# Attention's second product with stationary values and moving probabilities in a decoder layer on one Trainium2 core

## What is computed

```python
x = x + self_attention(layernorm(x))              # causal, 16 heads of 8 channels
x = x + cross_attention_mlp(layernorm(x), ctx)    # attention over 64 rows of ctx, then 128 -> 256 -> 128, relu
x = x + rotary_attention_moe(layernorm(x))        # rmsnorm, causal attention, then 2 of 8 experts
```

```python
attn = softmax(S, axis=-1)        # over the keys
out = attn @ V                    # [queries, 8], 16 heads side by side give 128 channels
```

## Time and profile before

| | us |
|---|---|
| median of 3 runs (lowest to highest) | 653.37 (652.38 to 659.31) |
| the profiled execution, its own time | 655.04 |
| its span in the profile | 653.1 |
| PE busy (PEld busy) | 584.1 (457.8) |
| DVE busy | 470.1 |
| ACT busy | 380.2 |
| POOL busy | 262.0 |

### The profile page before, as it was taken

How to read it: one execution, slowest core, us unless ns; L and a number is a source line. 1 busy time by engine, 2 the same in 40 slices (tenths; PEclk the granted TensorE clock), 3 DMA queues, 4 the chain that set the end, 5 groups by cost and what they waited for, 6 DMA issues and landing times.

```text
span 653.1 us, 29845 instructions
## 1 busy us (share of the span) xinstructions
PE 584.1 (89%) x12373; PEld 457.8 (70%) x12373; DVE 470.1 (72%) x1134; ACT 380.2 (58%) x759; POOL 262.0 (40%) x370
## 2 busy tenths in 40 slices
PE   3789999989999998799998989997689998999990
PEld 1556667667676676576766657665589998999990
DVE  4648788787879779779897989989746673333562
ACT  3445566655656756466756565554457666676750
POOL 6100101010122124246446375655417877754451
PEclk9789899999999999799999999998889999999995
DMA  5231413120100100001011001010122222432445
GB/s 129 74 93 58 128 32 105 27 89 11 39 12 18 32 21 31 23 15 44 24 39 36 27 23 33 32 40 14 45 71 72 63 82 71 111 100 64 137 146 173
DMA packets 45267, 38.98 MB, mean 60 GB/s; under 512 B 11552, under 2 KB 37728, under 8 KB 45136
## 3 DMA queue, kind: packets, MB, share of 16 engines
q1 hardware_dynamic: 36736, 24.22, 13.1%
q0 software_dynamic: 4320, 8.92, 4.1%
q10 hardware_dynamic: 4080, 3.93, 2.0%
HBM read 18.75 MB, written 12.01 MB: 47 GB/s over the span
## 4 chain that ended last, share of the span: by engine, by line
PE 52%; DVE 21%; issue 10%; POOL 10%; DMA 4%; ACT 2%; SPq 1%; POOLq 0%; ACTq 0%; DVEq 0%
PE ps_s L820 9%; PE ring L1193 8%; PE ring L1155 7%; DVE rmax L1379 6%; PE ps_s L1181 6%; DVE shifted L1383 5%; PE ring L1209 5%; PE ring L828 4%; POOL moved_dram L1583 3%; PE ring L1054 3%; PE ps_s L1168 2%; PE ring L1063 2%; PE ring L1135 2%; POOL y_dram L784 2%; DVE stats L1403 2%
## 5 line engine op out<-in xcount | busy, mean ns | idle before, releaser
L1240 ACT ACTIVATE probsT<-ring 128x512 f32<-128x512 f32 x192 | 104.7, 594 | 137.7 <-PE ring L1193 137.4
L1379 DVE TENSOR_REDUCE rmax<-ps_s 128x16 f32<-128x1024 f32 x96 | 117.2, 1221 | 25.4 <-PE ps_s L1181 24.7
L1383 DVE TENSOR_TENSOR shifted<-ps_s,rmax 128x1024 f32<-128x1024 f32 x96 | 117.6, 1225 | 9.8
L1193 PEld LDWEIGHTS ring<-const,shifted 128*128 128x128 f32 x768 | 85.2, 144 | 43.7 <-issue 41.8
L1193 PE MATMUL ring<-const,shifted 128*128 128x128 f32 x768 | 109.1, 286 | 5.3 <-DVE room L1469 3.2
L912 DVE TENSOR_TENSOR room<-room,ps_s 128x384 f32<-128x384 f32 x71 | 39.3, 554 | 78.9 <-PE ring L828 57.1
L784 POOL DMA_INDIRECT y_dram<-room x71 | 70.2, 989 | 61.4 <-DVE room L917 48.6
L1209 PEld LDWEIGHTS ring<-vbd,probsT 128*32 128x32 f32 x6144 | 63.9, 111 | 43.9 <-issue 28.9
L820 PE MATMUL ps_s<-room 128*128 128x128 f32 x648 | 83.0, 279 | 1.1 <-issue 0.8
L1209 PE MATMUL ring<-vbd,probsT 128*32 128x18 f32 x6144 | 73.1, 187 | 8.6 <-issue 5.8
L820 PEld LDWEIGHTS ps_s<-room 128*128 128x128 f32 x648 | 78.3, 195 | 1.7 <-issue 1.7
(11 more groups left out here) (187 smaller groups left out, 925.1 us busy)
## 6 DMA issues: line engine op xcount, KB each, us to landing
room<-kS SPq DMA_DIRECT2D x96, 64.0 KB
room<-moved_dram SPq DMA_DIRECT2D x71, 65.0 KB, 1.9
room<-y_dram ACTq DMA_DIRECT2D x10, 256.0 KB, 3.2
room<-in_x SPq DMA_DIRECT2D x8, 256.0 KB, 4.6
cin<-in_ctx SPq DMA_DIRECT2D x8, 192.0 KB, 3.4
w_exp<-in_L_ffn_wg SPq DMA_DIRECT2D x8, 192.0 KB, 2.8
w_exp<-in_L_ffn_wu SPq DMA_DIRECT2D x8, 192.0 KB, 3.2
w_exp<-in_L_ffn_wd SPq DMA_DIRECT2D x8, 192.0 KB, 3.4
```

Of the source, the lines that this page charges most:

```text
L1193: last = nc.tensor.transpose(ring[u.bank][:, k * P:(k + 1) * P], flat[:, c:c + P], ident)
L1240: nc.scalar.activation(probsT[p % 2][:, 4 * g:4 * g + 4, :], ring[u.bank][:].rearrange("p (k c) -> p k c", c=P), ACT.Exp, scale=SCALE)\
L1379: V.reduce_max(rmax[p % 2][:].rearrange("p (g k) -> p g k", g=GROUPS), ps_s, AX.X).then_inc(rmax_ready, 1)
L1383: V.tensor_tensor(shifted[p % 2][:].rearrange("p (g k) s -> p g k s", g=GROUPS), ps_s, rmax[p % 2][:].rearrange("p (g k) -> p g k", g=GROU ...
```

## The change

`probsT` becomes the moving operand and `vbd` the stationary one, so that the result comes out with channels on partitions. The 128 channels are four quarters of 32, each written by its own column tile of PE; a quarter holds four heads, two head pairs ("sides"). `vbd` has for each sequence and quarter a period of 48 columns: 16 of one side's values, 16 zeros, 16 of the other side's. A window of 32 columns from the start or from the middle holds one side's values and zeros for the other, and the two sides accumulate. The sums no longer come from a column of ones in the values but from a second set of products: `head_sums` has ones in the same pattern, so each channel's row gets its head's sum, once for each of its 8 channels. A bank then holds 128 columns of results and 128 columns of sums, both [channels, tokens]. DVE's reciprocal works on these 128 columns and the multiplication writes `oT` directly, which now has two buffers. The step oT goes, with its transposes and ACT's copy; wo, h0 and h1 wait for the last pair's multiplication. The bias bv is put into the MLP's bias once at the start: the step turn adds two products `w1.T @ bv`, and ACT adds b1 to them.

```diff
-VW = HEADS * (D + 1)
+PERIOD = 6 * D
+VW = HEADS // 4 * PERIOD
...
-    -1: {SELF: (((), ()), (("oT",), ("wo",)), ((), ()), ((), ())),
+    -1: {SELF: (((), ()), ((), ("wo",)), ((), ()), ((), ())),
...
-    oT = sb("oT", [P, TILE])
+    oT = [sb(f"oT{r}", [P, TILE]) for r in range(2)]
+    head_sums = sb("head_sums", [P, PERIOD])
...
-    rden = [sb(f"rden{r}", [P, HEADS]) for r in range(2)]
-    att = [sb(f"att{r}", [P, SUB, E]) for r in range(2)]
+    rden = [sb(f"rden{r}", [P, P]) for r in range(2)]
+    b1 = sb("b1", [P, 2])
...
-            elif name == "oT":
+            elif name in ("wo", "h0", "h1"):
                 drained(used("att", n, SUB - 1))
-            elif name in ("wo", "h0", "h1"):
-                drained(used("oT", n))
...
-                last = mm(ps_g[:, 2 * P:2 * P + 2], ident_slots[:], cols[:, 0:2], start=True, stop=True)
+                mm(ps_g[:, 2 * P:2 * P + 2], ident_slots[:], cols[:, 0:2], start=True, stop=True)
+                for k in range(2):
+                    last = mm(ps_g[:, 2 * P + 2 + k:2 * P + 3 + k], w1[:, k * P:(k + 1) * P], cols[:, 2:3],
+                              start=True, stop=True)
...
-            elif name == "oT":
-                last = transposes(ps_g, att[r])
...
-            for k in range(HEADS // 2):
-                c = 2 * (D + 1) * k
+            probs, by_head, sums = probsT[p % 2], ring[u.bank][:, 0:P], ring[u.bank][:, P:2 * P]
+            for b in range(2):
+                tok = slice(b * SEQ, b * SEQ + SEQ)
+                for side in range(2):
+                    for quarter in range(4):
+                        rows = slice(QUARTER * quarter, QUARTER * quarter + QUARTER)
+                        at = (2 * p + b) * VW + quarter * PERIOD + 2 * D * side
+                        mm(by_head[rows, tok], vbd[r][:, at:at + QUARTER], probs[:, 2 * quarter + side, tok],
+                           start=(side == 0), stop=(side == 1))
+            for side in range(2):
                 for quarter in range(4):
                     rows = slice(QUARTER * quarter, QUARTER * quarter + QUARTER)
-                    at = (2 * p + quarter // 2) * VW + c
-                    last = mm(ring[u.bank][rows, c:c + 2 * (D + 1)], probsT[p % 2][:, k, rows],
-                              vbd[r][:, at:at + 2 * (D + 1)], start=True, stop=True)
+                    last = mm(sums[rows], head_sums[:, 2 * D * side:2 * D * side + QUARTER],
+                              probs[:, 2 * quarter + side, :], start=(side == 0), stop=(side == 1))
...
-            elif name == "oT" and kind == CROSS:
-                ins = nc.scalar.activation(oT[:], ps_g[:], ACT.Identity, bias=cols[:, 2:3])
-            elif name == "oT":
-                ins = nc.scalar.activation(oT[:], ps_g[:], ACT.Copy)
...
-            o = ring[u.bank][:, 0:VW].rearrange("p (h c) -> p h c", h=HEADS)
-            V.reciprocal(rden[p % 2][:], o[:, :, D]).then_inc(rden_ready, 1)
+            V.reciprocal(rden[p % 2][:], ring[u.bank][:, P:2 * P]).then_inc(rden_ready, 1)
             dve.wait_ge(rden_ready, n * SUB + p + 1)
-            V.tensor_tensor(att[r][:, p, :].rearrange("p (h d) -> p h d", h=HEADS), o[:, :, 0:D],
-                            rden[p % 2][:].unsqueeze(2).broadcast_to([P, HEADS, D]), ALU.mult)\
+            V.tensor_tensor(oT[r][:, p * P:(p + 1) * P], ring[u.bank][:, 0:P], rden[p % 2][:], ALU.mult)\
              .then_inc(ring_drained[u.bank], 1)
```

More of the change, by code:

```diff
@@ L151 @@
         ROTARY: ((("q",), ("qr",)), ((), ("v",)), ((), ()), ((), ()))},
[L152 to L154 removed]
+    -1: {SELF: (((), ()), ((), ("wo",)), ((), ()), ((), ())),
+         CROSS: (((), ()), ((), ("h0",)), (("h1",), ()), (("ff",), ())),
+         ROTARY: (((), ()), ((), ("wo", "st2")), ((), ("ap2",)), ((), ("hT",)))},
     -2: {SELF: (((), ()), ((), ()), ((), ()), ((), ())),
@@ L220 @@
 TAIL_AT = {
-    -1: (("oT", LAST),),
     0: (("ta2", LAST), ("c0", LAST - 2)),
@@ L1127, in use @@
                 for s in range(SUB):
-                    last = mm(ps_g[:, s * P:(s + 1) * P], oT[:, s * P:(s + 1) * P], w, start=True, stop=True)
+                    last = mm(ps_g[:, s * P:(s + 1) * P], oT[r][:, s * P:(s + 1) * P], w, start=True, stop=True)
             elif name in ("h0", "h1"):
                 k = int(name[1])
-                last = mm(ps_g[:], w1[:, k * P:(k + 1) * P], oT[:], start=True, stop=True)
+                last = mm(ps_g[:], w1[:, k * P:(k + 1) * P], oT[r][:], start=True, stop=True)
             elif name == "ff":
@@ L1279, in values_out @@
             act.wait_ge(ring_filled, u.filled())
-            v = vbd[n % 2][:].rearrange("p (k c) -> p k c", c=2 * (D + 1))
-            ps = ring[u.bank][:].rearrange("p (k c) -> p k c", c=D)
+            v = vbd[n % 2][:].rearrange("p (k i c) -> p k i c", i=3, c=2 * D)
+            ps = ring[u.bank][:].rearrange("p (k i c) -> p k i c", i=2, c=D)
             for q in range(2):
                 rows = slice(SEQ * q, SEQ * q + SEQ)
-                last = nc.scalar.activation(v[rows, :, q * (D + 1):q * (D + 1) + D], ps[rows], ACT.Copy)
+                last = nc.scalar.activation(v[rows, :, 0:3:2, q * D:(q + 1) * D], ps[rows], ACT.Copy)
             last.then_inc(ring_drained[u.bank], 1)
@@ L1301, in use @@
                     nc.scalar.activation(bias_qk[:], ring[u.bank][:, 2 * P:2 * P + 2], ACT.Copy)
+                    for k in range(2):
+                        nc.scalar.activation(b1[:, k:k + 1], ring[u.bank][:, 2 * P + 2 + k:2 * P + 3 + k], ACT.Identity,
+                                             bias=cols[:, 3 + k:4 + k])
                 to = w_turned[:] if name == "turn" else w_f[:, 3:5, :]
@@ L1338, in use @@
                 k = int(name[1])
-                ins = nc.scalar.activation(h1T[:, k, :], ps_g[:], ACT.Relu, bias=cols[:, 3 + k:4 + k])
+                ins = nc.scalar.activation(h1T[:, k, :], ps_g[:], ACT.Relu, bias=b1[:, k:k + 1])
             elif name == "q":
@@ L1604, in _ @@
         for r in range(2):
-            last = G.memset(vbd[r][:], 0.0)
-        last.then_inc(pool_clear, 1)
+            G.memset(vbd[r][:], 0.0)
+        G.memset(head_sums[:], 0.0).then_inc(pool_clear, 1)
         pool.wait_ge(pool_clear, 1)
[L1608 to L1612, removed]
+        by_side = head_sums[:].rearrange("p (i c) -> p i c", c=2 * D)
+        for q in range(2):
+            last = G.memset(by_side[SEQ * q:SEQ * q + SEQ, 0:3:2, q * D:(q + 1) * D], 1.0)
         last.then_inc(pool_const, 1)
```

## The result

| | before | after |
|---|---|---|
| median of 5 runs each, us (lowest to highest) | 652.38 (649.94 to 659.31) | 681.13 (680.48 to 684.29) |
| ratio, 95% interval | | 1.041 (1.036 to 1.046) |
| the profiled execution, its own time | 655.04 | 684.29 |
| its span | 653.1 | 682.4 |
| DVE busy | 470.1 | 529.5 |

The change costs 28.7 us by the medians and 29.3 us by the two profiled executions. 43.9 us were predicted for the latter.

The account below looks back on a forecast made before the run. DVE was taken to set the pace in 40 of 94 attention pairs, PE in most others; 28.6, 8.4 and 6.5 us made 43.5, with +0.4 the profiled 655.0 became 698.9, or 697 us measured; range 670 to 725.

Parts of the forecast that it names:

- The reciprocal: On DVE, 128 elements instead of 16 per partition: 975 ns against 249, +0.73 us a pair, 70 us over 96 pairs.
- (a): DVE's reciprocal costs 8.3 ns an element, some 1.2 us each, +0.94 us a pair; 711 us measured; chance 0.14.
- (c): DVE's reciprocal streams one element a step, +0.04 us a pair, and PE's +0.19 counts nearly everywhere; 672 us; chance 0.10.
- The 40 pairs without a wait: Attention pairs with DVE waits under 0.1 us together: the reciprocal's 0.73 us counts, less that wait, 28.6 us.
- the 20 with a short one: Attention pairs with DVE waits between 0.1 and 0.54 us: what is left of 0.73 us counts, 8.4 us.
- PE's product: The second product on PE, as 8 rounds of 64 columns and 4 of 128 instead of 16: +0.35 us a pair.
- (b): PE's 64-column rounds cost four tiles only 0.037 us, net -0.15 us a pair; about 34 us more, 688; chance 0.08.
- (d): Only two column tiles of PE move at once, net +1.14 us in every pair; 107 us more, 761; chance 0.10.
- The transposes: The result's transposes leave PE: 0.63 us a job or 0.16 us a pair less, and 0.6 us once in the tail.
- the 34 others: Attention pairs with DVE waits above 0.54 us: DVE's extra fits in the wait, PE's net +0.19 us counts, 6.5 us.
- Small edits: POOL's larger clearing +0.5 us, four passes for the new bias +0.5, the tail's -0.6: +0.4 us together.
- (e): Not slower: streaming reciprocal on DVE and PE rounds at 0.037 us together give -4 us, 649 measured; chance 0.08.

Follow-up runs that it names:

- the kernel with 21 pauses: The kernel before with 16 tiny one-column products behind each pair's second product, 32 PE instructions a pair more; 691.3 us, ratio 1.050.
- the second profile of the changed kernel: The changed kernel run once more, nothing altered, beside the kernel before with the 128-element reciprocal; median 682.1 us, ratio 1.042.

## Why the prediction was right, and where its size was off

**The reciprocal: right.** 975 ns predicted, 946 measured, +0.70 us a pair and not +0.73. Its group rose by 67.0 us, DVE's busy time by 59.4, where some 70 were expected; why these two differ was not looked into. From 16 to 128 elements it is (949 - 257) / 112 = 6.2 ns an element, where 4 and 16 gave 6.4. Rivals (a) and (c) fall. The estimate of 8.3 ns from the page that the Trainium skill calls VectorE: DVE Perf Modes ("First, the fixed hardware budget") does not hold here, if its repeat count is read as clocks.

**DVE pays where it does not wait: right.** The 40 pairs without a wait gave +25.8 us (28.6 predicted), the 20 with a short one +6.2 (8.4). The wide reciprocal in the old kernel and the narrow one in the new show the same from both sides.

**PE's product: right in size.** +0.35 us where PE sets the pace, as worked out. So rivals (b), with its flat rounds, and (d), with its two tiles, fall; the time that (b) gave, 688, is nearer than 697, but not for its reason. The transposes: -7.0 us between the first and the last reciprocal by experiment, for 34 x 0.16 = 5.4. The 0.6 us of the tail did not show: behind the last reciprocal it is 181.3 us before and 181.6 without the transposes.

**What failed is the step "In the 34 others DVE's extra time fits in its wait, and PE's 0.19 counts: 6.5 us."** Measured: -7.3 us, 13.8 us under the step. The profiled time was missed by 14.6; the other misses, -2.8 and -2.2 us in the two classes above and +4.4 in the small edits, nearly cancel. The step took the waits of these pairs as PE's steady work. In four of them it was PE standing without a semaphore to wait for, by the runs above for lack of instructions, and a lower clock after that; with 32 instructions a pair fewer this went, 6.9 us of the 7.3, and it goes as well when the old kernel has fewer instructions and the old layout. The pauses stand in the trace of the kernel before, five of over 0.5 us with 5.8 us, and the prediction never asked about them. The "issue 10%" in the chain of the earlier trace rows does not measure them: it is some 65 us over all engines, and it is 8% in the kernel with 21 pauses and 7% in the one with none. Five more pairs (24, 41, 44, 54, 71) lost 3.3 us together; what their waits were I did not separate.

**Small edits.** +0.4 predicted; start and tail together came out at +4.8 us (first reciprocal 2.7 us later, 2.1 us more behind the last). In the second profile of the changed kernel the first reciprocal stands at 28.0 and not 30.5 us, so 2.5 us of it is that one execution's and not the change's.

**(e), not slower,** needed a reciprocal under 0.40 us.

## What to carry to other kernels

A result that comes out in a new layout changes the shape of every small operation on it: count free elements per partition for the one with the steepest slope, here a reciprocal at 6 ns an element, before weighing the matmuls. Where an engine's wait ends last, read what the engine waited for that one waits on: PE's pauses for nothing that the profile names were 5.8 us here, and they came and went with the number of its instructions. Setting each half of a change into the other kernel gives both prices with two runs.

## What the runs showed of the hardware

PE's instructions come in packets of 256: 32 a pair more are 12 packets more (101 to 113), 64 fewer are 24 fewer (101 to 77). A pause ends some 2.5 us after a packet's start. The old product with its 128 instructions a pair runs into this in five places (5.8 us), with 32 more in 21 (24.7 us), with 64 fewer in none of over 0.5 us. The Trainium skill (Runtime: NRT & Kernel Launch, "Instruction fetch mechanics") has blocks of 256 instructions as well, and says that their loading is mostly hidden because the sequencer is slower than the loading. These runs show the first and, by the reading above, a case in which the second does not hold.

A round of two column tiles of 64 takes 0.060 us with 18 columns moving, and 0.061 with 64; a round of four tiles of 32 takes 0.037 with 18 and 0.059 with 64. What bounds the first is then not the moving columns; the weight loads of 64 columns are longer (138 ns for 109), which may be it, but was not tried.
